# Latent attention: rotary partners swapped on VectorE instead of by DMA, QA and QB awaited apart, and the row sums of the last two query pairs kept on the core

## What is computed

```python
h = layernorm(x) * (1 + cb) + sb
xn = rmsnorm(h, w_ln1)
q = heads(xn @ Wq)                      # last 32 channels of a head are turned by _rope
ckv = xn @ Wkva; latent, k_rope = ckv[..., :32], ckv[..., 32:]
k = concat(heads(latent @ Wkvb), _rope(k_rope)); v = the unrotated part of k
att = softmax(causal(q @ k^T / 8))
h = h + (att @ v) @ Wo
# _rope, with channels in pairs: (x0, x1) -> (x0*cos - x1*sin, x0*sin + x1*cos)
```

## Time and profile before

| | |
|---|---|
| median of 3 runs | 2563.92 us (2563.19 to 2563.96) |
| the profiled execution, its own time | 2548.95 us |
| span in the profile, first to last instruction | 2547.2 us |
| the latent attention's main loop | 430 to 1456 us of the span |
| stretch before it, from the phase's first matmul | 384 to 430 us |
| stretch behind it, to the phase's last vector addition | 1458.8 to 1477.7 us |

### The profile page before, as it was taken

The page is one execution under the profiler, slowest core; times in us unless marked ns, Lnnn a source line. Parts: engine busy times, 40 slices in busy tenths (PEclk is TensorE's granted clock), DMA queues, the critical chain, the costliest instruction groups (busy, mean ns, idle before and its releaser), DMA issues. The chain is left out here.

```text
span 2547.2 us, 46473 instructions
## 1 busy us (share of the span) xinstructions
PE 2346.5 (92%) x16758; PEld 1948.6 (76%) x16758; DVE 1805.7 (71%) x3387; ACT 1376.2 (54%) x2609; POOL 934.2 (37%) x1044
## 2 busy tenths in 40 slices
PE   6998866999999999999999879999878888999999
PEld 5777754777778877787777768888767777888887
DVE  6888874897778777877787666666566558666664
ACT  5666543777777777777777743332334443333322
POOL 1233334364546454646444321121356641010100
PEclk9999987999999999999999989999989998999999
DMA  4011104443343345333443252332301112121221
GB/s 146 17 47 54 31 14 138 130 110 104 107 148 111 107 114 146 109 108 102 141 111 106 61 196 63 99 106 76 120 9 36 52 70 79 42 78 54 67 59 42
DMA packets 193076, 223.68 MB, mean 88 GB/s; under 512 B 37048, under 2 KB 156496, under 8 KB 189200
## 3 DMA queue, kind: packets, MB, share of 16 engines
q1 hardware_dynamic: 192848, 220.71, 30.2%
HBM read 150.75 MB, written 55.47 MB: 81 GB/s over the span
## 5 line engine op out<-in xcount | busy, mean ns | idle before, releaser
L1284 DVE TENSOR_REDUCE l_negmax<-l_mx 128x1 f32<-128x512 f32 (+3 forms) x608 | 393.3, 652 | 67.9 <-PE l_mx L1678 64.6
L1297 DVE TENSOR_TENSOR l_Plo<-l_s,l_Phi 128x512 fp32r<-128x512 f32 x576 | 391.4, 679 | 12.4 <-ACT l_s L1533 11.4
L1529 ACT ACTIVATE l_Phi<-l_s 128x512 fp32r<-128x512 f32 x576 | 338.9, 588 | 107.3 <-PE l_s L1702 105.6
L1533 ACT ACTIVATE l_s<-l_s 128x512 f32<-128x512 f32 x576 | 341.6, 593 | 0.0
L1678 PE MATMUL l_mx<-l_KK,l_QA 128*128 128x512 f32 (+3 forms) x768 | 281.0, 405 | 40.2 <-DMA l_QB<-l_qd 28.9
L1713 PE MATMUL l_o<-l_Phi,l_V 128*128 128x256 f32 x1152 | 302.4, 285 | 1.6 <-ACT l_Osb L1541 1.6
L2944 ACT ACTIVATE m_hidhi<-m_h 128x512 fp32r<-128x512 f32 x168 | 106.2, 632 | 358.6 <-DVE m_h L2753 358.6
L1713 PE MATMUL l_o<-l_Plo,l_V 128*128 128x256 f32 x1152 | 299.8, 282 | 0.0
L1700 PE MATMUL l_s<-l_QA,l_KK 128*128 128x512 f32 x576 | 250.4, 435 | 0.5 <-DMA l_QB<-l_mrow 0.3
L1713 PEld LDWEIGHTS l_o<-l_Phi,l_V 128*128 128x128 f32 x1152 | 219.1, 190 | 17.1 <-DVE l_Plo L1297 7.3
L1713 PEld LDWEIGHTS l_o<-l_Plo,l_V 128*128 128x128 f32 x1152 | 218.5, 190 | 15.8
(11 more groups left out here) (471 smaller groups left out, 6397.3 us busy)
## 6 DMA issues: line engine op xcount, KB each, us to landing
l_qd<-l_qs SPq DMA_DIRECT2D x256, 128.0 KB, 2.3
l_QA<-l_qd SPq DMA_DIRECT2D x64, 512.0 KB, 3.6
l_QB<-l_qd SPq DMA_DIRECT2D x64, 256.0 KB, 4.4
l_R<-l_rd SPq DMA_DIRECT2D x128, 128.0 KB, 2.9
m_spread<-m_combs SPq DMA_DIRECT2D x62, 256.0 KB, 5.2
kept<-m_combs SPq DMA_DIRECT2D x124, 128.0 KB, 4.9
xs<-next_store SPq DMA_DIRECT2D x32, 256.0 KB, 2.0
l_rps<-l_rp SPq DMA_DIRECT2D x128, 64.0 KB, 2.0
```

Source lines behind the costliest of these rows:

```text
L1284: v.tensor_reduce(negmax[:, n % 2, at + h0:at + h1], piece_of(number, chunk), AX.X, ALU.max, negate=True).then_inc(reduced, 1)
L1297: v.tensor_tensor(Plo[:, s % 3, x].rearrange("p h q -> p (h q)"), S2[s % 2][:, x * HALF:(x + 1) * HALF], Phi[:, s % 3, x].rearrange("p h q ...
L1529: a.activation(Phi[:, u // 2 % 3, u % 2].rearrange("p h q -> p (h q)"), scores_of(u), ACT.Exp, scale=L_D ** -0.5).then_inc(exped, 1)
L1533: a.activation(scores_of(u), scores_of(u), ACT.Exp, scale=L_D ** -0.5).then_inc(exped, 1)
```

## The change

Four edits, all in the latent attention:

1. `swap_query` and `swap_keys` leave SP's queue. They are now one `stream_shuffle` on DVE each, which permutes partitions within groups of 32. For queries it stands at i = 2, directly ahead of `query_low`; for keys at (12, 1) and (12, 7) of a batch.
2. qready is split into aready and bready. `maximum` waits for QA alone; the first `score` of a step waits for QB.
3. At the phase's start DVE's swaps and residuals stand ahead of its wait for the mask. SP's order of the remaining steps is as it was, `place_max` ahead of `store_query` as before.
4. For steps 62 and 63 (`local`), the sums don't go to DRAM. PE turns the rows of sums into columns of l_mx (`turn_sums`: matmuls of one column), DVE inverts them (`invert_here`), PE spreads them over 64 partitions in PSUM (`spread_inverse`: float32 matmuls of 128 columns), DVE multiplies (`divide_here`), ACT and DVE split (`half_high`, `low_here`), by halves of a step. `out_last` comes one unit sooner and takes the four steps in the order 60, 62, 61, 63.

The diff, cut to its core:

```diff
+    TURNED = {(STEPS - 1, 4): (STEPS - 2, 0, 8), (STEPS - 1, 8): (STEPS - 1, 0, 4)}
+    INVERTED = {(STEPS - 1, 6): (STEPS - 2, 0, 8), (STEPS, 0): (STEPS - 1, 0, 4), (STEPS, 4): (STEPS - 1, 4, 8)}
+    SPREAD = {(STEPS - 1, 6): (STEPS - 2, 0, 8), (STEPS, 1): (STEPS - 1, 0, 4)}
+    DIVIDED = {(STEPS - 1, 7): (STEPS - 2, 0), (STEPS - 1, 8): (STEPS - 2, 1), (STEPS, 2): (STEPS - 1, 0),
+               (STEPS, 5): (STEPS - 1, 1)}
...
-            def swap_query(d):
-                sp.wait_ge(qact, 2 * d + 1)
-                if d >= 2:
-                    sp.wait_ge(roped, d - 1)
-                for odd in range(2):
-                    sp.dma_start(rps[odd:P:2, d % 2], rp[1 - odd:P:2, d % 2]).then_inc(qswap[d % 2], 16)
...
-                             QD[d % 2].rearrange("c i h x -> (c i) (h x)")).then_inc(qready[d % 4], 16)
+                             QD[d % 2].rearrange("c i h x -> (c i) (h x)")).then_inc(aready[d % 4], 16)
                 sp.dma_start(QB[0:64, d % 4].rearrange("p h t q -> p (h t q)").bitcast(F32),
-                             QD[d % 2, 0:2].rearrange("c i h x -> (c i) (h x)"))\
-                    .then_inc(qready[d % 4], 16)
+                             QD[d % 2, 0:2].rearrange("c i h x -> (c i) (h x)")).then_inc(bready[d % 4], 16)
...
+            def swap_query(n):
+                v.wait_ge(qact, 2 * n + 1)
+                if n >= 2:
+                    v.wait_ge(roped, n - 1)
+                v.stream_shuffle(rps[:, n % 2].rearrange("p t q -> p (t q)"),
+                                 rp[:, n % 2].rearrange("p t q -> p (t q)"), swap).then_inc(qswap, 1)
...
+            def invert_here(n, r, lo, hi):
+                v.wait_ge(sums_turned, n + 1)
+                if lo == 0:
+                    v.wait_ge(rstored[r % 2], 16 * (r // 2))
+                v.reciprocal(rsum[:, r % 2, lo:hi], MX[:, lo:hi]).then_inc(local_inverse, 1)
+
+            def divide_here(r, t):
+                v.wait_ge(spread, L.part(r, t) if r == L.STEPS - 1 else 2)
+                for odd in range(2):
+                    rows = slice(64 * odd, 64 * odd + 64)
+                    v.tensor_tensor(Osb[rows, r % 3, t, 0:2 * P], Osb[rows, r % 3, t, odd * 2 * P:(odd + 1) * 2 * P],
+                                    inverse_bank(r, t)[rows, :], ALU.mult).then_inc(local_normal, 1)
...
                 if i == 2 and L.asks(m + 3):
+                    swap_query(m + 3)
                     query_low(m + 3)
...
+            def spread_inverse(turn, r, lo, hi):
+                pe.wait_ge(local_inverse, turn + 1)
+                if r == L.STEPS - 1:
+                    pe.wait_ge(lowered, UNITS * L.STEPS - 4 + hi // 4)
+                for n in range(lo, hi):
+                    t, odd, j = n // 4, n // 2 % 2, n % 2
+                    mm = pe.matmul(inverse_bank(r, t)[64 * odd:64 * odd + 64, j * P:(j + 1) * P],
+                                   rsum[:, r % 2, n:n + 1].broadcast_to([P, 64]), ident[:, :], start=True, stop=True,
+                                   skip_group_check=True)
+                    if n % 4 == 3:
+                        mm.then_inc(spread, 1)
...
                 if number == L.before(n):
-                    pe.wait_ge(qready[n % 4], 32 * (n // 4 + 1))
+                    pe.wait_ge(aready[n % 4], 16 * (n // 4 + 1))
...
                 if u % UNITS == 0:
+                    pe.wait_ge(bready[m % 4], 16 * (m // 4 + 1))
                     pe.wait_ge(mready[m % 2], 32 * (m // 2 + 1))
```

More of the change, by code:

```diff
@@ L889, in __init__ @@
                 for kind, key in self.bank_work(m, i):
-                    self.take(kind, key, 0 if (kind, key) == ("out", (self.STEPS // 4 - 1, 1)) else self.PJ_BANK)
+                    self.take(kind, key, 2 if (kind, key) == ("out", (self.STEPS // 4 - 1, 1)) else self.PJ_BANK)
     def take(self, kind, key, bank=PJ_BANK):
@@ L974, in scores, with local, part @@
         return [x for x in out if 0 <= x < self.STEPS * self.UNITS]
+    def local(self, r):
+        return r >= self.STEPS - 2
+    def part(self, r, t):
+        return 2 * (r - self.STEPS + 2) + t + 1
     def evacuated(self, u):
@@ L1039, in latent_attention @@
         khi, krope, klo, kdup, vhi = (signal(n) for n in ("khi", "krope", "klo", "kdup", "vhi"))
-        kswap = [signal(f"kswap{i}") for i in range(2)]
         scored, weighed, maxed, reduced = (signal(n) for n in ("scored", "weighed", "maxed", "reduced"))
@@ L1164, in _ @@
                 ahead = L.is_step(m) and b < B
-                if L.is_step(r):
+                if L.is_step(r) and not L.local(r):
                     sp.wait_ge(inverse, r + 1)
@@ L1170, in _ @@
                         .then_inc(rstored[r % 2], 16)
-                if ahead and ls in (12, 13):
-                    swap_keys(b, ls - 12)
                 if ahead and ls == 13:
                     double_keys(b, 0)
-                if L.asks(d):
-                    swap_query(d)
-                if L.is_step(c):
+                if L.is_step(c) and not L.local(c):
                     sp.wait_ge(evacuated, 2 * c + 2)
@@ L1312, in invert, with low_here @@
                 v.reciprocal(rsum[:, c % 2, :], sums[:, c % 2, :]).then_inc(inverse, 1)
+            def invert_here(n, r, lo, hi):
[9 more added lines that the diff above has]
+                                    inverse_bank(r, t)[rows, :], ALU.mult).then_inc(local_normal, 1)
+            def low_here(r, t):
+                v.wait_ge(yhigh, L.STEPS - 2 + L.part(r, t))
+                v.tensor_tensor(half_outputs(r, t, Ylo), half_normalized(r, t),
+                                half_outputs(r, t, Yhi).bitcast(F32), ALU.subtract).then_inc(local_low, 1)
+            swap = [i ^ 1 for i in range(32)]
+            swap_query(0)
+            query_low(0)
+            swap_keys(0, 0)
+            swap_keys(0, 1)
+            swap_query(1)
+            query_low(1)
+            value_low(0)
             v.wait_ge(mload, 16)
             v.tensor_copy(maskT[:, :], R[:, 1, 0, 0:P]).then_inc(consts, 1)
-            query_low(0)
-            query_low(1)
-            value_low(0)
             for m, i in steps:
                 u = m * UNITS + i
-                if i == 0 and L.is_step(m - 2):
+                if i == 0 and L.is_step(m - 2) and not L.local(m - 2):
                     invert(m - 2)
                 if i == 2 and L.asks(m + 3):
+                    swap_query(m + 3)
                     query_low(m + 3)
-                if i in (6, 8) and m % 4 == 2 and m >= 6:
+                if i in (6, 8) and m % 4 == 2 and 6 <= m < L.LAST:
                     add_out((m - 6) // 4, (i - 6) // 2)
@@ L1458, in _ @@
             for m, i in steps:
-                if i == 1 and L.is_step(m - 3):
+                if i == 1 and L.is_step(m - 3) and not L.local(m - 3):
                     outputs_low(m - 3)
@@ L1462, in _ @@
                     rope_queries(m + 3)
-                if i == 7 and L.is_step(m - 2):
+                if i == 7 and L.is_step(m - 2) and not L.local(m - 2):
                     normal_out(m - 2)
@@ L1547, in outputs_high, with half_high @@
                 a.activation(outputs(r, Yhi), normalized(r), ACT.Copy).then_inc(yhigh, 1)
+            def half_high(r, t):
+                a.wait_ge(local_normal, 2 * L.part(r, t))
+                if L.part(r, t) == 1:
+                    a.wait_ge(filled, L.use["out", (r // 4 - 1, 1)] + 1)
+                a.activation(half_outputs(r, t, Yhi), half_normalized(r, t), ACT.Copy).then_inc(yhigh, 1)
             a.wait_ge(lnload, 16)
@@ L1568, in _ @@
                 group = L.evacuated(u)
-                if i == 0 and L.is_step(m - 3):
+                if i == 0 and L.is_step(m - 3) and not L.local(m - 3):
                     outputs_high(m - 3)
```

87 lines of the change are left out of this document (66 added, 21 removed).

## The result

The changed kernel takes 2528.5 us (median of 4 executions, 2522.95 to 2531.87) against 2563.9 before (2563.19 to 2567.57): a ratio of 0.9874, with a 95% interval of 0.9856 to 0.9893. It is 35 us faster where 33 were forecast, inside the range of 2519 to 2546. Timed again on another chip it was 2528.8 against 2559.3: 30.5 us (0.9878, 0.9842 to 0.9915).

The account below looks back on a forecast made before the run. A chain through QB's load (14.7 us against PE's 13.7) bound plain steps not behind an output projection, DVE the statistics' steps. Start 3.3, main loop 23 and end 7 us summed to 33 off 2563.9: 2531 us, range 2519 to 2546.

Parts of the forecast that it names:

- QA awaited alone: Main loop, first maxima: each of 30 PE waits shrinks by up to 1.2 us; 25.4 us, 22.6 after the statistics' steps.
- the ring stays: Rival, main loop: QA lands hardly before QB, so the loop gains about 11 us; 2543 us in all; chance 0.13.
- PE's waits for DVE's maxima: Sign in the changed profile: growth of these waits from a few us to 10 would show the forecast wrong.
- Plain steps: Sign, main loop: steps without statistics come near 13.7 us, also where they took 14.3 to 14.7.
- The shuffle where DVE is full: About two loop steps per batch without spare DVE time: 8 x 0.40 = 3.2 us lost, half taken, 1.5 us.
- DVE takes over more widely: Rival: shuffles delay maxima in all statistics' steps and their neighbours; the loop gains 14 us, 2540 in all; chance 0.09.
- The clock: TensorE's clock in the main loop: shorter PE waits mean less time at the lower level, 2 us gained, bounds 0 and 4.
- The rotation ends sooner; nothing: POOL's rotation, main loop: ends earlier by the swap's landing, but in most steps is ready when SP stores; worth nothing.
- The loop: Main loop of the latent attention: 22.6 - 1.5 + 2.0 = 23 us gained.
- The start: Before PE's first maximum: POOL's waits of 2.66 and 0.60 us for swapped rows go; 3.3 us gained, bounds 0 and 3.3.
- The end: Last weigh to last addition takes 8 us instead of 18.9, the last weigh comes 4.5 later; 7 us gained with clock.
- more than the rows show: Rival: the timed runs' extra 15 us is clock lost behind PE's waits; another 10 us gained, 2521 us; chance 0.10.

Follow-up runs that it names:

- e1: The kernel before with QA and QB counted on two semaphores, nothing else changed: 2536.1 us, ratio to before 0.9905.
- e7: The changed kernel with query swaps by DMA again in the 15 statistics steps alone: 2520.9 us, ratio to before 0.9847.
- e2: The kernel before with the swaps as shuffles on DVE, nothing else changed: 2546.0 us, ratio to before 0.9945.
- e5: The kernel before with shuffles, plus DMAs at the swaps' old queue place copying cosines to an unread buffer: 2554.6 us, ratio to before 0.9985.
- e12: The changed kernel with all swaps back on DMAs, split semaphores and local sums kept: 2529.5 us, ratio to before 0.9892.
- e8: The changed kernel again, unaltered, timed on another chip: 2528.8 us, ratio to before 0.9878.
- e9: The changed kernel with the doubling DMA of the next batch's second key half issued ahead of QA's and QB's loads: 2525.5 us, ratio to before 0.9877.
- e3: The kernel before with the local sums of tiles 62 and 63, nothing else changed: 2554.8 us, ratio to before 0.998.
- e4: The changed kernel with QA and QB counted on one semaphore again: 2542.9 us, ratio to before 0.9931.
- e6: The changed kernel with a second shuffle into a spare buffer ahead of each of the loop's 62: 2536.7 us, ratio to before 0.9907.
- e10: The changed kernel with tile 62's sums back through DRAM and its output products last: 2525.8 us, ratio to before 0.9883.
- e11: The changed kernel with the edits of e7, e9 and e10 together: 2519.4 us, ratio to before 0.9857.

## Why the prediction held, point by point

- **QA awaited alone.** Borne out. PE's wait for the load at first maxima fell from 28.9 us in 30 waits to 3.1 in 5: 25.8 us against the 25.4 of the term, and under the 6 named. QB still lands 1.1 us behind QA, and no score waits for it. The rival "the ring stays" fell with e1. The 2.8 us set aside for the statistics' steps were misread: nine of the 30 waits lie in steps 4 to 9 of the first three batches, 5.9 us together; at 513, 562 and 1082 PE idled for under 0.1 us, and 1294 lies in the last batch, which has no statistics.
- **PE's waits for DVE's maxima.** Their growth to 10 us was named as a sign of being wrong, and it came: 4.1 us before, 5.8 + 4.3 after. It isn't the shuffle's doing alone: e1, which has none, shows 7.9 + 3.3.
- **Plain steps.** Partly as forecast: 1, 17, 33 and 49 had 13.84 to 14.67 us and have 13.84, but 16, 48 and 60 still take 15.01, 14.40 and 14.30 (before 15.84, 15.44, 17.62).
- **The shuffle's own time.** 0.443 us at the median where 0.47 was worked out, 0.34 from start to start where I had 0.40.
- **The shuffle where DVE is full: mis-sized.** The term was 1.5 us (8 steps by 0.40, halved); e7 measures 4.3 us over the 15 statistics steps. The halving was an error, and the unhalved 3.2 is short too: the output step behind did not even it out, and step 7 pays as well (7, 23 and 39: 13.66 before, 13.89 after, 13.67 in e7). The rival "DVE takes over more widely" was right in direction, at under half its 10 us.
- **The port between DVE and POOL.** The 64 shuffles take 432 to 454 ns, and 12 of them ran beside a POOL instruction; none took longer for it. The Trainium skill (SBUF — State Buffer, "SBUF: two separate sides") has the pair of ports that DVE and POOL share locked by a DVE operation only in a 2-port mode or with two SBUF inputs. The trace agrees, as far as 12 cases go.
- **The clock.** Right in kind, a little small: the loop's granted clock went from 0.99 to 1.00. The two stretches at the lower level, in steps 37 and 60, are gone, and these steps take 14.23 and 14.30 us instead of 16.90 and 17.62. That is 2 x 1.7 = 3.4 us where the term had 2.
- **"The rotation ends sooner; nothing": the step that failed.** It was judged by "most steps". In 8 of 59 steps the rotation was last, which the trace of before had in a row of SP's queue (6.6 us, shown above). e2 measures 15.6 us for the swap alone, where the terms for the swap came to some 2 (3.3 for the start, less 1.5). The late rotation isn't all of it, since e5 lost most of the gain without one; how the gain divides between rotation and DMA traffic stays open. It cost the forecast little only because the split takes the same waits away: with it made, the swap has 1 to 4 us left in the loop (e1 and e12). Nor was it true that the shuffle is worth nothing to the chain because SP's wait at the sums' store grows: the wait did grow (141.5 to 304.1 us), and the chain behind it still got shorter.
- **The loop.** 20.4 us against 23. By the terms as measured: 25.8, less the 6.0 by which the waits for maxima grew, less 4.3 for the shuffles, plus 3.4 for the clock, 18.9. The terms overlap (a wait for maxima can be the shuffle's), so this is a check of size, not a split.
- **The start.** 3.0 us of the 3.3. POOL's first rotation starts right behind its casts (399.16), and the whole phase began 2.2 us later in this execution. The second execution of the changed kernel (e8) has 27.26 us too, but e7 and e9, whose start is the same, have 30.42 and 29.12: their projections ran longer at the lower clock and came last. So the 3 us are there when nothing else is late.
- **The end: mis-sized by the clock.** The tail is 7.9 us where 8 was worked out. Step 63 grew by 5.6 us, not by 4.5, and the gain is 5.4 us, not 7. ACT idled 1.20 and 2.58 us behind turns and spreads, as these rows of the changed kernel show; the third row is the spreads in e3.

```profile
1431.13 1.84 PE L1722 MATMUL l_mx<-ident,l_Osb 128*128 128x1 f32 x16
...
1434.88 2.03 PE L1732 MATMUL l_mx<-ident,l_rsum 128*64 128x128 f32 x16
```

```profile
1464.10 1.14 PE L1733 MATMUL l_mx<-ident,l_rsum 128*64 128x128 f32 x16
```

```profile
1434.13 0.60 ACT L1585 ACTIVATE l_Phi<-l_s 128x512 fp32r<-128x512 f32 x1 [1.20 <-PE l_s L1798]
...
1437.80 0.60 ACT L1585 ACTIVATE l_Phi<-l_s 128x512 fp32r<-128x512 f32 x1 [2.58 <-PE l_s L1798]
```

The turns took 1.84 us instead of 1.3. The spreads, put at 2.1, took 2.03 in the changed kernel but 1.14 in e3 and e4, and the difference is the granted clock, here in the changed kernel during the spreads and in e3:

```profile
1434.88:1436.91 2.03, 2.03 (x18) 1.70 (x17) 0.69 (x1) 0.34 (x1) 0.00 (x0) 0.50 0.00 0
1464.10:1465.25 1.15, 1.15 (x18) 0.98 (x17) 0.40 (x1) 0.72 (x2) 0.00 (x0) 1.00 0.00 0
```

In e3 and e4 the clock stayed at 1.00 through step 63, which took 16.92 us; in after, e6, e8 and e12 it lay at 0.50 for 3.4 us, and the step took 18.43 to 18.45; in e7 and e9 for 6.8 us, and it took 19.98. So the new work costs step 63 4.1 us at full clock, a little under the 4.5 worked out, and each 3.4 us at the lower level cost 1.5 more. With the clock at 1.00 the end gains 6.9 us (e3), the 7 of the forecast. The clock did not fall in step 63 in e10 and e11, which lack tile 62's turns and spreads, nor in e3 and e4, which have them. What decides it isn't shown.

- **The sum against the median: near by luck.** The stages give 28.4 us, not 33, and yet the median fell by 30 to 35. The forecast took the same 33 us off both. The difference lies in before: its profiled execution (2549) is below all 38 timed ones (2550.4 to 2568.2), while the changed kernel's lie at 2523 to 2532. Most of that difference is the clock, as the rival "more than the rows show" supposed. Each execution's mean granted clock is on record, and its span times one minus that clock is an estimate of the time lost to the lower level (good to about 1 us, as the clock has three digits). Its median is 81.8 us in 34 executions of before, whose clocks are 0.964 to 0.972, and 67.0 us in the 8 of the changed kernel, at 0.971 to 0.976. That is 15 of the 30 us between their median spans (2557.3 and 2527.1). Before's traced execution, 10 us below that median, lost 74 us, 8 fewer. The seven longest executions of before had 0.964 to 0.966, the seven shortest 0.967 to 0.972. In the same way the split alone (e1) saves 4 us of clock and 17 of other time, the swap alone (e2) 8 and 5. The kernels that wait for QA and QB together and have a swap's DMAs in SP's queue (before, e3, e5) spread over 10 to 17 us, all others, with fewer executions, over 2 to 9. In the traced executions the loop loses 3.4 us to the lower level in before and none in the changed kernel. In which steps the longest executions lose theirs stays open, since none of them was traced.

## What to carry to other kernels

A wait on two loads under one semaphore is worth splitting when only the first is needed, and the wait row bounds the gain: 28.9 us of waiting gave 19 in the loop. When judging who ends last at a join, count the steps in which each side does, not the usual step: the mean cost sits in the few others. And work moved onto an engine with spare time on average is paid in the stretches in which it has none; there the old way can be kept, which here was worth 5 us in the loop and 8 in the median (e7). And PE's time for new work depends on the granted clock that it meets: the same 16 spreads took 1.14 us or 2.03.
